# Routed experts: gates in the rows' headers, gated outputs added by scatter into the output, no summing stage

## The reference

```
n  = layer_norm(h)                                  # h: the stream so far
x  = n + attention(layer_norm(n))
xn = layer_norm(x)                                  # 4096 tokens
top_logits, top_idx = top_k(xn @ gate_w, 2)         # of 8 experts
gates = softmax(top_logits)                         # two per token
y_e   = gelu(xn @ w1[e] + b1[e]) @ w2[e] + b2[e]    # hidden width 768
out   = h + x + sum over the token's two experts of gate * y_e
```

## Time and profile before

| | |
|---|---|
| time, median of 3 runs | 2379.43 us (2377.87 to 2382.93) |
| span of the profiled execution | 2403.1 us |
| PE busy | 1879.3 us (78%) |
| DVE busy | 1495.5 us (62%) |
| ACT busy | 1074.7 us (45%) |
| POOL busy | 395.9 us (16%) |
| last row of an expert tile sent, to the end of the span | 2371.8 to 2403.1 us |

### The profile page before, as it was taken

The page is one execution under the profiler, slowest core; times in us unless marked ns, Lnnn a source line. Parts: engine busy times, 40 slices in busy tenths (PEclk is TensorE's granted clock), DMA queues, the critical chain, the costliest instruction groups (busy, mean ns, idle before and its releaser), DMA issues. The chain is left out here.

```text
span 2403.1 us, 30974 instructions
## 1 busy us (share of the span) xinstructions
PE 1879.3 (78%) x9780; PEld 1007.5 (42%) x9804; DVE 1495.5 (62%) x2518; ACT 1074.7 (45%) x1896; POOL 395.9 (16%) x595
## 2 busy tenths in 40 slices
PE   3868788858876453777668877998899984999994
PEld 2745655535333320000022234442133333888883
DVE  4558449966010687999878876999788883111114
ACT  1100222214110476999979964342477661222220
POOL 5000000000112010222100003331033343222221
PEclk8989999968887575555589978997799996999997
DMA  3011110005797004443011008777666703566664
GB/s 85 1 39 31 48 31 27 20 10 229 309 411 314 20 0 127 127 127 123 18 32 40 26 16 119 130 132 107 83 88 95 97 28 135 195 201 203 202 203 184
DMA packets 147792, 264.98 MB, mean 110 GB/s; under 512 B 28864, under 2 KB 115985, under 8 KB 142678
## 3 DMA queue, kind: packets, MB, share of 16 engines
q1 hardware_dynamic: 135750, 242.10, 38.0%
q0 software_dynamic: 10768, 18.19, 2.3%
q10 hardware_dynamic: 1152, 3.15, 0.3%
HBM read 221.85 MB, written 57.71 MB: 116 GB/s over the span
## 5 line engine op out<-in xcount | busy, mean ns | idle before, releaser
L1743 PE MATMUL ps<-arena 128*128 x376 | 194.9, 621 | 108.2 <-ACT ps L1785 60.1
L1785 ACT ACTIVATE ps<-ps,arena 128x512 f32<-128x512 f32 x384 | 256.7, 1121 | 6.3 <-POOL arena L1769 6.3
L1753 DVE TENSOR_REDUCE arena<-ps 128x1024 f32 x192 | 232.8, 1225 | 24.5 <-PE ps L1743 12.2
L1785 ACT ACTIVATION_READ_ACCUMULATOR ps<-ps,arena 128x1 f32 x384 | 234.7, 668 | 0.0
L2159 DVE TENSOR_REDUCE arena<-ps 128x1024 f32 x192 | 221.3, 1219 | 12.4 <-PE ps L2405 9.8
L2618 ACT ACTIVATE arena<-ps 128x1024 f32<-128x1024 f32 x192 | 185.1, 1020 | 97.6 <-PE ps L2500 96.4
L2962 DVE TENSOR_TENSOR arena<-ps,arena 128x384 f32<-128x384 f32 x39 | 21.8, 558 | 286.4 <-PE ps L2918 286.4
L2942 ACT ACTIVATE arena<-ps,arena 128x256 f32<-128x256 f32 x234 | 89.5, 481 | 235.9 <-PE ps L2907 230.0
L2405 PE MATMUL ps<-arena 96*128 96x512 bf16 x500 | 162.7, 430 | 26.4 <-DVE arena L2159 12.2
L1950 ACT ACTIVATE arena<-ps 128x1024 f32<-128x1024 f32 x192 | 178.7, 1048 | 7.8 <-DVE arena L1970 4.6
L529 PE MATMUL ps<-arena 96*128 96x456 f32 (+1 forms) x512 | 170.3, 482 | 8.8 <-DMA arena<-la_xt 5.2
(11 more groups left out here) (394 smaller groups left out, 3264.8 us busy)
## 6 DMA issues: line engine op xcount, KB each, us to landing
arena<-in_sm_w_dram SPq DMA_DIRECT2D x128, 576.0 KB, 15.5
arena<-in_re_w_dram SPq DMA_DIRECT2D x39, 1252.0 KB, 5.9
arena<-ra_parts SPq DMA_DIRECT2D x192, 192.0 KB, 9.1
routed_in<-routed_in SPq DMA_DIRECT2D x8, 3332.0 KB, 14.2
ra_parts<-arena SPq DMA_DIRECT2D x48, 192.0 KB, 2.4
arena<-routed_in SPq DMA_DIRECT2D x39, 196.0 KB, 5.4
arena<-la_xt SPq DMA_DIRECT2D x16, 384.0 KB, 3.4
arena<-arena SPq DMA_DIRECT2D x64, 96.0 KB, 2.2
```

The costliest lines, as they stand in the source:

```text
L1743: ins = pe.matmul(ps[:, 2 * (n % 4) + t % 2, :], QM[j][:, h, t * P:(t + 1) * P], KI[:, b, h // HG, :], start=True, stop=True)
L1753: v.tensor_reduce(MXq[:, b, 2 * u:2 * u + 2, at_head(h)], ps[:, 2 * (n % 4):2 * (n % 4) + 2, :], AX.X, ALU.max).then_inc(s_lk, 1)
L1785: ins = act.activation(bank, bank, ACT.Exp, bias=nb[n % 4][:, t % 2:t % 2 + 1], scale=c_reg, accum_out=RS[:, b, t, at_head(h):at_head(h) + 1])
```

## The change

The header now carries all that the receiver needs: word 0 is the token's own row of the output (the same in both copies), word 1 is the gate of the second expert, word 2 the first gate minus the second, and word 3 the number of the first expert. GpSimd computes the gates of a batch before it sends its rows (`gap`, `gates`), with ACT's exponential between (`gap_exp`, in the next batch but one behind exponential 7). DVE writes word 3. There is no second header for the second copy and no copied rows for the last batch.

In a tile, DVE picks the gate by comparing word 3 with the tile's expert (`m.TEf`), multiplies b2 by it ahead of the output, and moves the output out of PSUM with two instructions of 192 columns in place of one of 384. The scatter has `compute_op=ALU.add` and goes into `io.out`. SP has stored the stream `m.H` there before: batches 0 to 5 during the attention stage, batches 6 and 7 behind the loads of the first two tiles' rows. GpSimd waits for these stores before its first scatter. The summing stage and `routed_out` are gone. `io.out` has 256 more rows, to which padding rows are added; they are cut off on return.

```diff
+            def store_stream(sp, p):
+                lc.wait(sp, p, 1)
+                sp.dma_start(out_rows(p), m.H[:, p, :, :]).then_inc(m.stored, 16)
+
...
                 shift_rows(sp, b)
-
+                if b > 2:
+                    store_stream(sp, b - 3)
+
+            store_stream(sp, B - 3)
             av.wait(sp, B - 1, NS)
...
+            store_stream(sp, B - 1)
 
         @block.tensor
...
+            def gap_exp(p):
+                act.wait_ge(s_d, p + 1)
+                act.activation(GD, GD, ACT.Exp).then_inc(s_e, 1)
+
...
+                    if b > 1 and e == 7:
+                        gap_exp(b - 2)
+            gap_exp(B - 2)
...
-            act.wait_ge(s_sc[1], 16 * T * (B - 1))
-            act.wait_ge(s_gb, 2 * B)
-            act.activation(XA[B % 2][:, :, HEAD:RW], XA[1 - B % 2][:, :, HEAD:RW], ACT.Copy).then_inc(s_gb, 1)
-            act.wait_ge(s_d, 1)
-            act.activation(d, d, ACT.Exp).then_inc(s_e, 1)
+            gap_exp(B - 1)
...
                 gr.wait(v, p, 1)
                 if p > 1:
...
                 gate(ins)
...
+            v.tensor_scalar(m.TEf, TF, NX - 1.0, None, ALU.min)
...
-            v.tensor_tensor(d, VM[:, :, 1], VM[:, :, 0], ALU.subtract).then_inc(s_d, 1)
-            v.wait_ge(s_e, 1)
-            gate(v.tensor_scalar(m.GT[:, :, 1], d, 1.0, None, ALU.add))
-            gate(v.reciprocal(m.GT[:, :, 0], m.GT[:, :, 1]))
-            gate(v.tensor_tensor(m.GT[:, :, 1], m.GT[:, :, 0], d, ALU.mult))
...
-            def send(p, k, source=None):
-                a = p % 2 if source is None else source
-                pool.iota(to_row[a], [[1, T]], base=k * NT * P + p * S, channel_multiplier=T).then_inc(s_ir, 1)
-                pool.wait_ge(s_ir, 2 * p + k + 1)
-                pool.wait_ge(s_gb, 2 * p + 2)
-                po.wait(pool, p, 1)
-                if source is not None:
-                    pool.wait_ge(s_gb, 2 * p + 3)
+            def gap(p):
+                mk.wait(pool, p, 1)
+                pool.tensor_tensor(GD, VM[:, p * T:p * T + T, 1], VM[:, p * T:p * T + T, 0], ALU.subtract).then_inc(s_d, 1)
+
+            def gates(p):
+                head = XA[p % 2]
+                pool.iota(to_row[p % 2], [[1, T]], base=p * S, channel_multiplier=T)
+                pool.wait_ge(s_e, p + 1)
+                pool.tensor_tensor(G0, GD, m.one.to_broadcast([P, T]), ALU.add).then_inc(s_hd, 1)
+                pool.wait_ge(s_hd, 4 * p + 1)
+                pool.tensor_tensor(G0, G0, minus1, ALU.pow).then_inc(s_hd, 1)
+                pool.wait_ge(s_hd, 4 * p + 2)
+                pool.tensor_tensor(head[:, :, 1], GD, G0, ALU.mult).then_inc(s_hd, 1)
+                pool.wait_ge(s_hd, 4 * p + 3)
+                pool.tensor_tensor(head[:, :, 2], G0, head[:, :, 1], ALU.subtract).then_inc(s_hd, 1)
+
+            def send(p, k):
+                if k == 0:
+                    pool.wait_ge(s_hd, 4 * p + 4)
+                    pool.wait_ge(s_gb, 2 * p + 2)
+                    po.wait(pool, p, 1)
...
                     pool.indirect_dma_start(xd, bass.IndirectOffsetOnAxis(ap=POS[p % 2][:, k, t:t + 1], axis=0),
-                                            XA[a][:, t, :], None).then_inc(s_sc[k], 16)
+                                            XA[p % 2][:, t, :], None).then_inc(s_sc[p % 2], 16)
...
-            for p in range(B - 1):
+            for p in range(B):
+                gap(p)
+                gates(p)
                 send(p, 0)
-                rstd(p + 1)
-                pool.wait_ge(s_sc[0], 16 * T * (p + 1))
+                if p + 1 < B:
+                    rstd(p + 1)
                 send(p, 1)
                 if p + 1 < B - 1:
                     scale(p + 1)
-            pool.wait_ge(s_sc[1], 16 * T * (B - 1))
-            send(B - 1, 0)
-            send(B - 1, 1, B % 2)
...
+            pool.wait_ge(m.stored, 16 * B)
...
-                    pool.indirect_dma_start(yd, bass.IndirectOffsetOnAxis(ap=back[n % 4][:, h:h + 1], axis=0),
-                                            YM[j][:, h, :], None).then_inc(m.ym[j], 16)
+                    pool.indirect_dma_start(io.out, bass.IndirectOffsetOnAxis(ap=back[n % 4][:, h:h + 1], axis=0),
+                                            YM[j][:, h, :], None, compute_op=ALU.add).then_inc(m.ym[j], 16)
                 pool.wait_ge(m.ym[j], 32 * (n // 2 + 1))
                 pool.sem_inc(yf.sem, 1)
...
+                head = XM[n % 2]
+                v.tensor_copy(back[n % 4], head.bitcast(I32)[:, :, 0])
+                link(v.scalar_tensor_tensor(out=GN[n % 4], in0=head[:, :, 3], scalar=m.TEf[:, n:n + 1], in1=head[:, :, 2],
+                                            op0=ALU.is_equal, op1=ALU.mult))
+                v.tensor_tensor(GN[n % 4], GN[n % 4], head[:, :, 1], ALU.add)
                 hp.wait(v, n, -3)
                 v.tensor_copy(XT[n % 2].rearrange("p c q -> p (c q)"), ps[:, 0, :]).then_inc(xc.sem, 1)
 
             def out(n):
+                gate = GN[n % 4]
+                hp.wait(v, n, 1)
+                b2 = WR[n % NW][:, B2_AT:B2_AT + D]
+                for h in range(2):
+                    ins = v.tensor_scalar(YB[n % 2][:, h, :], b2, gate[:, h:h + 1], None, ALU.mult)
+                link(ins)
                 yp.wait(v, n, 1)
                 yf.wait(v, n, -1)
-                b2 = WR[n % NW][:, B2_AT:B2_AT + D]
-                v.tensor_tensor(YM[n % 2], ps[:, 7, 0:2 * D].rearrange("p (h d) -> p h d", h=2),
-                                b2[:, None, :].to_broadcast([P, 2, D]), ALU.add).then_inc(yc.sem, 1)
+                for h in range(2):
+                    ins = v.scalar_tensor_tensor(out=YM[n % 2][:, h, :], in0=ps[:, 7, h * D:(h + 1) * D],
+                                                 scalar=gate[:, h:h + 1], in1=YB[n % 2][:, h, :], op0=ALU.mult, op1=ALU.add)
+                ins.then_inc(yc.sem, 1)
 
...
-    Y = Cut(m.arena, R_AT, E_AT)(P, [B, 2, T, D])
...
-            for b in range(B):
-                v.wait_ge(s_g[b], 32)
-                for k in range(2):
-                    for t in range(T):
-                        ins = v.scalar_tensor_tensor(out=m.H[:, b, t, :], in0=Y[:, b, k, t, :],
-                                                     scalar=GT[:, T * b + t, k:k + 1], in1=m.H[:, b, t, :],
-                                                     op0=ALU.mult, op1=ALU.add)
-                    if k:
-                        ins.then_inc(s_f, 1)
-                    else:
-                        link(ins)
...
-        @block.sync
-        def _(sp):
-            for b in range(B):
-                for k in range(2):
-                    at = (k * B + b) * S
-                    sp.dma_start(Y[:, b, k, :, :], rows_of(yd[at:at + S])).then_inc(s_g[b], 16)
...
-        @block.scalar
-        def _(act):
-            for b in range(B):
-                act.wait_ge(s_f, b + 1)
-                act.dma_start(rows_of(io.out[b]), m.H[:, b, :, :]).then_inc(s_o, 16)
-            act.wait_ge(s_o, 16 * B)
-
```

More of the change, by code:

```diff
@@ L2846, in routed_experts @@
     back = [w(P, [2], I32) for _ in range(4)]
+    GN = [w(P, [2]) for _ in range(4)]
+    YB = two([2, D])
     xm = m.xm
@@ L3075 @@
                                            kind="ExternalInput").ap()
-    io.out = nc.dram_tensor("out_0_dram", (B, S, D), F32, kind="ExternalOutput").ap()
+    io.out = nc.dram_tensor("out_0_dram", (NT * P + TR, D), F32, kind="ExternalOutput").ap()
     kernel_program(nc, io)
     r = run_bass_kernel_spmd(nc, [arrays], core_ids=[0])
-    return r.results[0]["out_0_dram"]
+    return r.results[0]["out_0_dram"][0:NT * P].reshape(B, S, D)
```

34 lines of the change are left out of this document (14 added, 20 removed).

## The result

The changed kernel takes 2358.28 us (median of 4, 2355.66 to 2358.76), the kernel before beside it 2381.14 (2377.87 to 2382.93): ratio 0.9906, interval 0.9878 to 0.9933. By the ratio that is 22 us less (16 to 29 by the interval; 22.9 between the medians); 20.3 were predicted. A second set of runs of the same kernel (last experiment) gave 0.9878, 0.9849 to 0.9908, that is 29 us (22 to 36).

The account below looks back on a forecast made before the run. PE was taken to bound the tiles, DVE the 31.3 us behind the last tile. Terms: 26.9 - 0.6 - 1.4 - 4.0 - 0.6 = 20.3 us gained, so 2379.4 - 20.3 = 2359.1 us, range 2353 to 2366 (chance 0.72).

Parts of the forecast that it names:

- Removed: 31.3 us: Program's end: the whole stretch behind the last scatter goes, 31.3 us, of which 26.9 us remain as net gain.
- The addition in the DMA: Program's end: adding in the last scatter lengthens its landing by 1.5 us, between 0 and 2.6.
- The tiles: 0.6 us lost: Last two tiles: DVE's longer output costs 2 x 0.2 us, scatter 38's wait for scatter 37 another 0.2.
- far over 0.96 us: Sign of being wrong: a scatter's issue on GpSimd taking far more than the 0.96 us it took before.
- In all other tiles a slower scatter has room: Expert tiles: GpSimd's round, 2.2 us of issue plus landing, exceeds the tile's 8.63 us only with landings over 6.4 us.
- the scatter becomes the bound: Rival, expert tiles: additions can't overlap, landings over 6.4 us (0.4 us a row) lengthen 38 tiles; 2430 us, chance 0.09.
- Change of stage: 1.4 us lost: Between attention and experts: two store issues on SP cost 1.0 us, two gate operations before the first row copy 0.35.
- The attention batches: 4.0 us lost: Batches 2 to 7: DVE's copy of word 3 costs 1.0 us, DVE held up by GpSimd's new power 3.0.
- DVE's L2720 would be held some 0.5 us: Attention batches: GpSimd's new power runs beside this DVE operation and delays it, 6 x 0.5 = 3.0 us.
- The copy's 0.17 us a batch: Attention batches: DVE's copy of header word 3 lengthens the chain PE waits for, 0.17 x 6 = 1.0 us.
- the batches pay for the gates: Rival, attention: DVE held for all GpSimd's small operations, or ACT's exponential late; 13 us for 3, 2369 us, chance 0.13.
- End of the attention stage: 0.6 us lost: Last batch: gates delay the first send by 0.9 us, the dropped header between sends gives back 0.3.

Follow-up runs that it names:

- e2: The changed kernel with its scatter overwriting rows of the output in place of adding to them; 2352.03 us, ratio 0.9897 to the kernel before.
- e4: The changed kernel with a 576-column memset (0.58 us) on GpSimd in each tile before it signals the buffer free; 2356.45 us, ratio 0.9896.
- e5: The changed kernel with a 1440-column memset (1.30 us) on GpSimd in each tile before it signals the buffer free; 2359.23 us, ratio 0.9928.
- e9: The changed kernel with two 1440-column memsets in a row on GpSimd in each tile before the buffer is signalled free; 2389.33 us, ratio 1.0026.
- e8: The changed kernel with batch 6's store ahead of SP's wait for the last exponentials, batch 7's behind the experts' first loads; 2353.78 us, ratio 0.9899.
- the change again: The changed kernel unedited, measured a second time beside the kernel before; 2352.36 us, ratio 0.9878.
- e3: The changed kernel without computing gates: GpSimd's five operations and ACT's small exponential gone, header words 1 and 2 zero; 2353.34 us, ratio 0.9896.
- e1: The kernel before without its summing stage: stream stored as in the change, experts' rows scattered plainly to their own buffer, never added; 2352.5 us, ratio 0.9891.
- e7: The changed kernel with GpSimd waiting between a batch's two sends for the first to land and rewriting the header there; 2352.7 us, ratio 0.9902.
- e6: The changed kernel with SP loading a tile's weights when an earlier scatter has landed, not when its output is copied; 2353.88 us, ratio 0.9901.
- e10: The changed kernel with the edits of e6 and e8 together; 2357.0 us, ratio 0.9903 to the kernel before.

## Why the prediction was right, and which terms were not

The mechanism was right: the stage behind the last scatter goes, and the tiles stay bound by PE. That the time came within 1 us is luck in part. By the traces the gain is 27.3 us against 20.3: 28.7 at the end, less 2.5 in the tiles, less 0.4 between ranks and first tile, plus 1.4 in the batches (rounded), where the prediction had 26.9 - 0.6 - 2.0 - 4.0. Too much put down for the batches stood against too little for the tiles. By its own steps:

- **Removed: 31.3 us.** Right. Net, I put 26.9; it is 31.34 - 2.61 = 28.7. "The addition in the DMA" was put at 1.5 us between 0 and 2.6, and measures 0.5 (e2). The landing, meeting and end of program, 1.67 + 1.2 = 2.9, measure 2.1 with a plain scatter.
- **The tiles: 0.6 us lost.** 2.5 lost. The output did grow by 0.2 us (0.74 for 0.56) and PE's wait at tile 37 by 0.24, as said. What I had no term for is the scatter's issue on GpSimd, 1.55 for 0.96 us: two of them at the end are 1.2. And scatter 38 waited not 0.2 but 1.0 us for scatter 37, for the same reason: the issues of 37 ended 1.2 us later. The time from there to the next issue was put at 2.8 us and is 2.70, 1.9 of landing and 0.8 until GpSimd goes on. A price of the issue "far over 0.96 us" was named as a sign of being wrong; 1.55 is that sign, and it cost 2.2 us.
- **In all other tiles a slower scatter has room.** The result holds, the reason is weaker than I wrote. The round is 1.85 us from first to second issue, some 6.0 to the landing and 0.8 to the next issue: 8.6 to 8.7 us, at the bound of 8.62, not below it. It doesn't set the pace because the landing gives way (e4, e5) and because two output buffers let GpSimd lag. The rival "the scatter becomes the bound" had its threshold about right; e9 shows it passed, at 2.7 us more of GpSimd's time. By the Trainium skill, DMA: Bandwidth & Descriptors, section "Two DMAs through the same engine are not ordered", neighbouring read-modify-writes overlap. The trace agrees: the last scatter has 128 rows, 8 for each of 16 DMA engines if they are spread evenly, and its landing came only 0.5 us later than without the addition (e2), far from the 0.4 us a row that the rival needed.
- **Change of stage: 1.4 us lost.** Both terms are right, and yet PE's first tile starts 11.06 us behind the last send's start, where it was 11.03 before, not some 2 us later. The stores' 1.0 is 0.9 (e8). The gate picks' 0.35 is 0.32: PE waits 1.27 us for the second copy of turned rows in place of 0.95. It falls into the first tile, where a granted clock of 0.64 in place of 0.60 over the first 10 us hides it. The stores were hidden by a quicker landing behind the last send: 4.3 us in the change and 4.7 in the change again, 5.1 before.
- **The attention batches: 4.0 us lost.** This step failed. "DVE's L2720 would be held some 0.5 us" by the power: it wasn't, and e3 puts the gates at 0.5 us or less in all. The step read a conflict of operations of 512 and 768 columns into one of 4 columns. The copy's 0.17 us a batch hardly shows either: e1 has neither gates nor copy, and its batches take 33.47 to 33.55 us, within 0.1 of the change's; PE's wait before the ranks is 0.70 us there and 0.78 in the change, not 1.4. The other rival, "the batches pay for the gates", fell with it. The Trainium skill, SBUF — State Buffer, section "Who interferes with whom", has the first engine hold the shared ports for its whole instruction. The trace agrees one way (L2811 waits out L2734) and not the other: the power started 0.63 us ahead of L2734 and held up nothing.
- The batches at the full clock even got shorter, 33.5 to 33.6 us for 33.6, 33.9 and 34.0. The part of it that is visible is the operation beside `scale`, 1.39 for 1.89 us in the middle batches, as `scale` starts 0.5 us earlier against it. Why it starts earlier I can't say: neither the gates (e3) nor the wait between the sends (e7) moves it, and e1, which has the sends and headers of before, is as quick. What e1 and the change share and the kernel before lacks is SyncE's stores of the stream and the missing last block. No run parts the two, and of the kernel before there is one trace. This stays open, for 1.4 us or so.
- **End of the attention stage: 0.6 us lost.** From ranks to the first send it is 2.99 us in place of 2.33: 0.66, with 0.3 back for the header, as worked out. But it doesn't reach PE. Counted from the ranks the first row load comes at 17.80 us in the change and 18.20 in the change again, 18.33 before and 18.35 in e3. The runs that send at 2.33 us (before, e1, e3) have landings of 5.1 to 5.4 us behind the last send, those that send at 2.93 to 2.99 have 4.3 to 4.7 (e7 apart, whose sends wait in between): the landing gives back what the gates took. The two loads of weights that are issued 7.0 us behind the ranks in the change and in e3 alike would explain it; no run moved them.

## What to carry to other kernels

- A last stage that only gathers and sums, with nothing beside it, can be taken into the scatters that feed it. Here 31.3 us went and some 4 came back. Price the new transfer by its issue on the engine that sends it first: it grew by 0.6 us each time, and at the end of the chain that was more than the longer landing (0.5).
- A wait put down to the producer can hide a second one. Compare the gap behind the producer's end with what it was (0.28 us against 0.80). Then load the suspected engine step by step; one step of 0.6 us would have shown too little here, and two of 1.3 showed the edge.
- Where a landing is long, see what is issued beside it. Moving one load away from the scatter cut the landing from 6.2 to 4.4 us and gave back all the room, at no cost in e6; in e10 the same edit came with waits for rows and 2.2 us lost.

## What was not expected of the hardware

- An indirect DMA that adds, of 128 rows of 768 bytes, takes 1.55 us of GpSimd's time, one that writes 0.96, with three times the packets (8059 for 2689 in 240 us) for the same 5.5 MB.
- The landing of such a scatter (from the start of its issue) depends on when the other loads start: from 3.4 to 3.7 us in the last tiles, which have none beside them, about 6 with a load of 1252 KB issued at the same moment, 4.0 to 8.5 with that load issued 1.3 us behind it (e9).
- A power of 128x4 on GpSimd (1.06 us) did not hold VectorE's 128x768 addition of two SBUF operands, which took 0.96 us beside it in six of six batches, as it does without it. GpSimd's next small operation, behind the addition's start, was held to 0.49 to 0.52 us in place of 0.20.
